# Half the memsets between gathers, one broadcast load of edge numbers, and 14 more kept blocks in a graph layer on one core

## The reference

```
edge_in_f = concat(h[src], h[dst], edge_attr)        # 192 wide
edge_in_r = concat(h[dst], h[src], edge_attr)
msgs_f = relu(edge_in_f @ W1_f + b1_f) @ W2_f + b2_f # 128 wide
msgs_r = relu(edge_in_r @ W1_r + b1_r) @ W2_r + b2_r
agg = segment_sum(msgs_f, dst, N) + segment_sum(msgs_r, src, N)
out = x + h + relu(concat(agg, h) @ Wn1 + bn1) @ Wn2 + bn2
```

## Time and profile before

| | us |
|---|---|
| median of three runs | 1631.61 |
| lowest, highest | 1625.42, 1633.73 |
| the profiled execution | 1627.22 |
| its span, first to last instruction | 1625.5 |
| busy in it: PE, DVE, ACT, POOL | 1318.5, 972.4, 944.0, 1120.1 |

### The profile page before, as it was taken

The page is one execution under the profiler, slowest core; times in us unless marked ns, Lnnn a source line. Parts: engine busy times, 40 slices in busy tenths (PEclk is TensorE's granted clock), DMA queues, the critical chain, the costliest instruction groups (busy, mean ns, idle before and its releaser), DMA issues.

```text
span 1625.5 us, 29085 instructions
## 1 busy us (share of the span) xinstructions
PE 1318.5 (81%) x7070; PEld 997.1 (61%) x7070; DVE 972.4 (60%) x2902; ACT 944.0 (58%) x2256; POOL 1120.1 (69%) x1003
## 2 busy tenths in 40 slices
PE   6988998457787788887877887878888865899998
PEld 4777776345565666665656665656666654666665
DVE  7999998336666666666665666666666641222222
ACT  5888888244555455555545555455555533677776
POOL 7899878888888888888888888888888862000000
PEclk9999999567878777778787778787777777999999
DMA  7999998335555555555545555555555546999998
GB/s 222 310 312 315 315 312 280 101 59 108 103 109 108 107 104 103 102 103 103 102 93 99 101 103 102 98 100 102 103 103 102 102 76 205 333 369 348 346 349 292
DMA packets 238374, 280.71 MB, mean 173 GB/s; under 512 B 53170, under 2 KB 155200, under 8 KB 238348
## 3 DMA queue, kind: packets, MB, share of 16 engines
q1 hardware_dynamic: 168408, 241.57, 44.7%
q0 software_dynamic: 68992, 38.59, 20.3%
q10 hardware_dynamic: 948, 0.30, 0.1%
HBM read 162.62 MB, written 117.72 MB: 172 GB/s over the span
## 4 chain that ended last, share of the span: by engine, by line
POOL 28%; issue 19%; DMA 15%; PE 9%; DVE 5%; ACT 1%; POOLq 0%; SPq 0%; DVEq 0%; another core or an unknown queue 0%; ACTq 0%
POOL table L532 24%; DMA out_x<-ncentred 12%; POOL got_odd L514 5%; DMA table<-to_send,scatter_at 3%; PE bank L846 3%; DVE ncentred L1137 2%; PE bank L820 2%; PE bank L818 2%; PE bank L833 1%; DVE same L979 1%; PE bank L871 1%; DMA same<-table 1%; PE bank L804 1%; PE bank L882 0%; DVE sums L961 0%
## 5 line engine op out<-in xcount | busy, mean ns | idle before, releaser
L532 POOL DMA_INDIRECT table<-to_send,scatter_at x392 | 640.9, 1635 | 134.1 <-issue 118.3
L846 PEld LDWEIGHTS bank<-message,same 128*128 128x128 f32 x1960 | 300.1, 243 | 47.1 <-issue 43.6
L846 PE MATMUL bank<-message,same 128*128 128x128 f32 x1960 | 322.4, 335 | 3.3 <-DVE message L1010 3.3
L639 ACT ACTIVATE nh<-nx,all_sums,all_rstd 128x64 f32<-128x64 f32 x784 | 280.2, 434 | 0.0
L514 POOL DMA_INDIRECT got_even<-in_x,gather_first x196 | 211.8, 1081 | 40.9 <-issue 36.1
L775 PE MATMUL bank<-wn_h,nturned 128*128 128x256 f32 x784 | 196.6, 394 | 26.9 <-ACT nhidden L683 18.4
L514 POOL DMA_INDIRECT got_odd<-in_x,gather_at x180 | 179.9, 999 | 54.8 <-issue 54.2
L818 PE MATMUL bank<-turned,w_ends 128*128 128x256 f32 x392 | 175.5, 540 | 37.8 <-ACT turned_edge L609 37.1
L804 PE MATMUL bank<-ident,h_ends 128*128 128x128 f32 x196 | 51.4, 355 | 184.4 <-DVE h_ends L1019 181.4
L1004 DVE TENSOR_TENSOR scatter_at<-moved,ids 128x4 int32<-128x4 f32 x98 | 16.0, 163 | 296.6 <-DMA table<-to_send,scatter_at 296.6
L775 PEld LDWEIGHTS bank<-wn_h,nturned 128*128 128x128 f32 x784 | 143.1, 192 | 63.3 <-issue 33.0
(11 more groups left out here) (78 smaller groups left out, 1971.0 us busy)
## 6 DMA issues: line engine op xcount, KB each, us to landing
nx<-in_x SPq DMA_DIRECT2D x194, 256.0 KB
table<-nhidden SPq DMA_DIRECT2D x97, 512.0 KB
same<-table SPq DMA_DIRECT2D x97, 512.0 KB, 5.3
others<-numbers SPq DMA_DIRECT2D x196, 128.0 KB
out_x<-ncentred SPq DMA_DIRECT2D x97, 256.0 KB, 4.4
nx<-out_x SPq DMA_DIRECT2D x55, 256.0 KB, 4.6
out_x<-nh SPq DMA_DIRECT2D x31, 256.0 KB
table<-to_send,scatter_at POOLq DMA_INDIRECT x392
```

The lines of the kernel that those rows point to most:

```text
L532: pool.indirect_dma_start(table, bass.IndirectOffsetOnAxis(ap=scatter_at[s][:, k:k + 1], axis=0), to_send[s][:, k, :], None, compute_op=AL ...
L639: last = act.activation(nh[s][:, g, :], nx[place][:, g, :], ACT.Relu, bias=all_sums[:, at, g:g + 1].rearrange("p a g -> p (a g)"), scale=a ...
L846: last = pe.matmul(bank[6 + s][:, k * M:(k + 1) * M], same[s][:, o, k * P:(k + 1) * P], message[s][:, o, :], start=(o == k), stop=(o == KB ...
```

## The change

Three things change, and buffers are laid over each other to make room.

- Pauses: the memset stands only behind every second gather of those issued ahead, 104 times in place of 208, and `copy_sums` waits for 104.
- Edge numbers: `numbers` is laid out tile by tile, the 128 sources and then the 128 targets of each tile, so that a batch's row is 512 numbers in one piece; `others` is loaded by one DMA of 256 KB in place of two of 128 KB.
- Kept blocks: place 3 as before (24), place 1 for all 24 full turns, place 2 for turns 16 to 23 (THIRD = 8): 56 windows. Stored and loaded again are 42: place 0 (25), place 2 for turns 0 to 15, and window 97.
- Buffers: `kept_more` grows from 18 to 32 slots of 2 KB per partition. For room, ncentred, nsquares, nturned and the rows for `table` (now `nrows`) lie in slots 12 to 21 of it in the first stage, and `zeros` in slots 8 and 9. In the third stage nhidden, nbiased (nturned before) and nout lie over buffers of the second stage. ends_int and ends_row lie over others[1] and message[0], for which SP waits once more (`s_rowf`).

```
-    MORE = 18
-    MORE_FROM = KEPT - MORE
+    THIRD = 8
+    THIRD_FROM = KEPT - THIRD
...
-    numbers = nc.dram_tensor("numbers", (2, NT * P), I32, kind="Internal").ap()
+    numbers = nc.dram_tensor("numbers", (NT, 2, P), I32, kind="Internal").ap()
...
-        nxh = [nh[2], nh[3], nsquares[0]]
+        nxh = [nh[2], nh[3], nh[3]]
...
-        kept_more = sb("kept_more", [P, MORE, G * D])
-        zeros = kept_more[:, 0:2, :].rearrange("p a c -> p (a c)")[:, 0:ZC]
-        nturned = two("nturned", [G // 2 * P])
-        nhidden = two("nhidden", [G * P])
-        nout = ncentred
+        kept_more = sb("kept_more", [P, KEPT + THIRD, G * D])
...
+        zeros = kept_more[:, 8:10, :].rearrange("p a c -> p (a c)")[:, 0:ZC]
+        ncentred = [kept_more[:, 12 + s, :].rearrange("p (g d) -> p g d", d=D) for s in range(2)]
+        nsquares = [kept_more[:, 14 + s, :].rearrange("p (g d) -> p g d", d=D) for s in range(2)]
+        nturned = [kept_more[:, 16 + s, :] for s in range(2)]
+        nrows = [kept_more[:, 18 + 2 * s:20 + 2 * s, :].rearrange("p a c -> p (a c)") for s in range(2)]
...
         def in_ring(w, k):
 
-            place = w.of(NRING, k)[1]
-            return not (place == NRING - 1 or place == 1 and MORE_FROM <= w.least(k) // NRING < KEPT)
+            place, turn = w.of(NRING, k)[1], w.least(k) // NRING
+            return place == 0 or place == 1 and turn >= KEPT or place == 2 and turn < THIRD_FROM
...
-                for end in (SRC, DST):
-                    sp.dma_start(others[s][:, :, end, :],
-                                 numbers[end:end + 1, bass.ds(first_edge, JT * P)]
-                                 .rearrange("a (j p) -> a j p", p=P).to_broadcast([P, JT, P])
-                                 ).then_inc(s_others[s], 16)
+                sp.dma_start(others[s][:, :, :, :].rearrange("p j e q -> p (j e q)"),
+                             numbers.rearrange("(a t) e p -> a (t e p)", a=1)
+                             [:, bass.ds((2 * i + s) * (KB * P), KB * P)].to_broadcast([P, KB * P])
+                             ).then_inc(s_others[s], 16)
...
                     sp.wait_ge(s_numbers, 32)
+                    sp.wait_ge(s_rowf, 1)
                     load(0, 0)
...
                     else:
                         continue
+                    if k % 2 == 0:
+                        continue
                     if pauses:
                         pool.wait_ge(s_paused, pauses)
                     pool.memset(idle, 0.0).then_inc(s_paused, 1)
...
                 elif s == 0:
-                    act.wait_ge(s_paused, KB * (PAIRS + LOOK))
+                    act.wait_ge(s_paused, KB // 2 * (PAIRS + LOOK))
...
-                    if not first(turn):
-                        dve.wait_ge(e_stored[place], 16 * (turn - skipped(w, k)))
+                    if place == 1:
+                        dve.wait_ge(e_stored[2], 16 * THIRD_FROM)
+                    elif not first(turn):
+                        dve.wait_ge(e_stored[place], 16 * turn)
```

More of the change, by code:

```diff
@@ L166, in gnn_layer @@
         sums = two("sums", [KB])
-        centred = two("centred", [KB, D])
-        squares = two("squares", [KB, D])
+        moments = two("moments", [2, KB, D])
+        centred = [moments[s][:, 0, :, :] for s in range(2)]
+        squares = [moments[s][:, 1, :, :] for s in range(2)]
         var = two("var", [KB])
@@ L183, in gnn_layer @@
         to_send = two("to_send", [KB, M])
+        ends_int = others[1][0:TB, :, :, :]
+        ends_row = message[0][0:TB, :, :].rearrange("p (e b) q -> p e b q", b=2)
         nx = [sb(f"nx{p}", [P, G, D]) for p in range(NRING)]
@@ L191, in gnn_layer @@
         all_rstd = sb("all_rstd", [P, NW, G])
-        ncentred = two("ncentred", [G, D])
-        nsquares = two("nsquares", [G, D])
         nvar = two("nvar", [G])
@@ L196, in gnn_layer @@
         nh = [sb(f"nh{p}", [P, G, D]) for p in range(NRING)]
-        nxh = [nh[2], nh[3], nsquares[0]]
+        nxh = [nh[2], nh[3], nh[3]]
         idle = to_send[0][:, 0:2, :].rearrange("p k m -> p (k m)")
-        kept_more = sb("kept_more", [P, MORE, G * D])
-        zeros = kept_more[:, 0:2, :].rearrange("p a c -> p (a c)")[:, 0:ZC]
-        nturned = two("nturned", [G // 2 * P])
-        nhidden = two("nhidden", [G * P])
-        nout = ncentred
+        kept_more = sb("kept_more", [P, KEPT + THIRD, G * D])
[4 more added lines that the diff above has]
+        nrows = [kept_more[:, 18 + 2 * s:20 + 2 * s, :].rearrange("p a c -> p (a c)") for s in range(2)]
+        nhidden = [[to_send[s][:, :, :].rearrange("p k m -> p (k m)"),
+                    moments[s][:, :, :, :].rearrange("p a k d -> p (a k d)")] for s in range(2)]
+        nbiased = [hidden[s][:, :, :].rearrange("p a b -> p (a b)") for s in range(2)]
+        nout = [message[s][:, :, :].rearrange("p k (h d) -> p (k h) d", d=D) for s in range(2)]
         s_params = sem("params_in")
@@ L349, in set_up @@
                 for end in (SRC, DST):
-                    sp.dma_start(numbers[end, :].rearrange("(b t p) -> t b p", b=2, p=P),
+                    sp.dma_start(numbers[:, end, :].rearrange("(b t) p -> t b p", b=2),
                                  ends_int[:, end, :, :]).then_inc(s_numbers, 16)
@@ L410, in store_rows @@
                 sp.wait_ge(b_rows[s], 2 * (i + 1))
-                store_window(table[0:N, :], i, s, nhidden[s][:, :], b_stored[s])
+                store_window(table[0:N, :], i, s, nrows[s], b_stored[s])
             def begin(w):
@@ L450, in batch @@
                 store_xh(w, -1)
-            run(sp, NB, [(4, MORE_FROM * NRING, 4), (MORE_FROM * NRING, 92, 4)], 1, batch)
+            run(sp, NB, [(4, THIRD_FROM * NRING, 4), (THIRD_FROM * NRING, 92, 4)], 1, batch)
             def load_xh(w, k):
@@ L471, in store @@
                 store_window(out, i, s, flat(nout[s]), n_stored[s])
-            for place, turns in ((0, KEPT + 1), (1, KEPT + 1 - MORE), (2, KEPT)):
+            for place, turns in ((0, KEPT + 1), (1, 1), (2, THIRD_FROM)):
                 sp.wait_ge(e_stored[place], 16 * turns)
@@ L675, in copy_begin @@
                     act.wait_ge(b_product[s], i)
-                act.copy(nturned[s][:, :], bank[s][:, :]).then_inc(b_turned[s], 1)
+                act.copy(nturned[s], bank[s][:, :]).then_inc(b_turned[s], 1)
             def copy_rows(half):
@@ L682, in copy @@
                         act.wait_ge(b_stored[s], 16 * i)
-                    act.copy(nhidden[s][:, half * 512:(half + 1) * 512], bank[2 + 2 * s + half][:, :]
+                    act.copy(nrows[s][:, half * 512:(half + 1) * 512], bank[2 + 2 * s + half][:, :]
                              ).then_inc(b_rows[s], 1)
@@ L719, in add_bias @@
                     act.wait_ge(n_back[s], i)
-                act.activation(nturned[s][:, :], bank[s][:, :], ACT.Identity,
+                act.activation(nbiased[s], bank[s][:, :], ACT.Identity,
                                bias=bn2_col[:, 0:1]).then_inc(n_biased[s], 1)
@@ L882, in layer2_nodes @@
                         last = pe.matmul(bank[s][odd * D:(odd + 1) * D, c:c + 256], wn2[:, :],
-                                         nhidden[s][:, odd * 512 + c:odd * 512 + c + 256], start=True, stop=True)
+                                         nhidden[s][odd][:, c:c + 256], start=True, stop=True)
                 last.then_inc(n_l2[s], 1)
@@ L891, in turn_back @@
                 for q in range(G // 2):
-                    last = pe.transpose(bank[6 + s][:, q * P:(q + 1) * P], nturned[s][:, q * P:(q + 1) * P], ident[:, :])
+                    last = pe.transpose(bank[6 + s][:, q * P:(q + 1) * P], nbiased[s][:, q * P:(q + 1) * P], ident[:, :])
                 last.then_inc(n_back[s], 1)
```

23 lines of the change are left out of this document (11 added, 12 removed).

## The result

| | us |
|---|---|
| kernel before, median of 4 runs | 1629.58 (1625.42 to 1633.73) |
| changed kernel, median of 4 runs | 1816.10 (1811.87 to 1818.96) |
| ratio | 1.114, 95% interval 1.110 to 1.118 |
| profiled execution of the changed kernel | 1811.87, span 1810.1 |

The forecast was 1594. The changed kernel is 11% slower, outside the range and in a way that none of the rivals had. That is half of the result. The other half came with the last runs: **the same file, not altered by a letter, took 1590.34 us when it was run again, on chip 5** (4 runs, 1585.76 to 1593.63, against 1628.39 there; ratio 0.977, 0.975 to 0.979). The chip of the first measurement is not on record.

What follows compares the result with a forecast made beforehand. VectorE paces the first stage, POOL's queue the edge stage, DMA engines are 0.95 busy in the last; POOL's pauses delay the first scatter. Pauses 31.6 plus loads 5.7 save 37.3 us: 1594.3 us from the 1631.61 median, range 1582 to 1612.

Steps and rivals of the forecast that it cites:

- Part 1: First stage, POOL's gathers issued ahead: 208 memsets become 104, saving 31.6 us (19.8 pauses, 11.8 gathers hit less often).
- the pauses "0" below: Lower bound on the halved pauses' gain: 0 if the gap between gathers in the first stage is 0.49 us.
- Rival D: First stage: paired gathers block VectorE's two-input instructions, 0.48 us each, delaying the join; 50 us slower, 1682 us; chance 0.04.
- Gaps of 0.30 us, pauses at 0.19 us net: First-stage gathers: a pause occupies 0.49 us, 0.30 remains without it, so 104 removed pauses save 19.8 us.
- Gathers that meet VectorE: First stage: gathers lengthened by a running VectorE instruction are hit less often with the new step, saving 11.8 us.
- the walk: Gathers stepped along VectorE's recorded instructions: last pause ends at 307.4 us with the new sequence, 339.0 with the old.
- the bound of 37.3 us: Most that the pauses can give: first join done at 302.0 us, last pause ends at 339.3.
- Merged load: 0: Edge stage: 196 issues of 128 KB become 98 of 256 KB, hidden behind POOL, costed at nothing.
- 14 more kept blocks: 5.7: Last stage: 13 loads fewer at 0.44 us each save 5.7 us, bounds 2 and 13.4; the 14 stores saved give nothing.
- the forecast's quarter load (0.109): Last stage: a quarter of a load less per window is worth 0.109 us, from paces of 2.712 and 2.603 us.

Runs made afterwards that it cites:

- i1_changed_again: The changed kernel, not altered, run again in a later group on chip 5: 1590.34 us, ratio 0.9767 to the kernel before.
- e2_half_only: The kernel before with only the pauses halved (memset behind every second gather issued ahead), on chip 9: 1598.05 us, ratio 0.9788.
- h4_best: The changed kernel without pauses, edge ends in own buffers, 54 blocks kept, on chip 5: 1590.34 us, ratio 0.9757 to the kernel before.
- e1_all_pauses: The changed kernel with the memset again behind every gather (208), all other edits left in, on chip 9: 1626.76 us, ratio 0.9972 to the kernel before.
- i2_half_again: The kernel before with only the pauses halved, run again beside the changed kernel on chip 5: 1597.64 us, ratio 0.9805.
- f3_none: The changed kernel with no pause at all behind the gathers issued ahead, on chip 8: 1844.72 us (one run), stalled.
- f4_short_all: The changed kernel with a short memset (128x8) behind every gather, on chip 8: 1820.82 us, ratio 1.116 to the kernel before, stalled.

## Why the prediction was right and wrong

**The step that failed** in the measurement on record is the end of Part 1: "VectorE, TensorE and the loads have already gone as far as they can. The stage behind is the same chain started 31.6 us earlier." It priced a pause by POOL's time alone (0.49 us, 0.19 net) and took the first join to be done at 302 us whatever POOL does. In the stalled trace that join was done at 521.97 us, because the windows before it waited for TensorE's held increments, and the first scatter came at 523.45 us, not 309. In the trace of before, with 0.49 us behind every gather, no increment of TensorE was late in the first stage; that the pauses were the reason is argued, not shown, since half of them did no harm on chips 9 and 5. The trace of before could not give that price; but the prediction bounded the pauses "0" below, without asking whether a gap on one engine is a resource of another. **Rival D** had the right question (gathers in pairs block an engine of the first stage) and the wrong engine, VectorE, with a price from its own instructions. They didn't lengthen: 681 and 696 ns before, 681 and 706 in i1_changed_again, 683 and 697 for those that ran in the first 277 us of the stalled trace, means of the two groups of two-input instructions. The Trainium skill's rule (SBUF — State Buffer, Who interferes with whom), read as D reads it, that a GpSimd instruction which starts first holds up VectorE's, isn't seen in any of them; the other direction, a gather held up by VectorE, is the earlier trace rows. What D lacked is that an engine can be blocked between its instructions, in the signal that it is done.

Term by term, with i1_changed_again beside the kernel before (spans 1584.0 and 1625.5, so 41.5 us; forecast 37.3):

- **Gaps of 0.30 us, pauses at 0.19 us net: right.** The last pause ended 37.8 us sooner (339.3 to 301.5), of which the gathers' own time, below, is 18.1; 19.7 are left for the pauses, where 19.8 were forecast. The timeline of the end of the gathers:

```profile
298.69 1.07 POOL L525 DMA_INDIRECT got_even<-in_x,gather_first  x1 [0.16 <-issue]
300.06 0.97 POOL L525 DMA_INDIRECT got_even<-in_x,gather_first  x1 [0.30 <-issue]
300.27 2.50 PE L859 MATMUL bank<-message,same 128*128 128x128 f32 x20
...
301.03 0.45 POOL L580 MEMSET to_send<- 128x256 f32 x1
...
302.80 0.59 ACT L638 COPY to_send<-bank 128x512 f32<-128x512 f32 x1 [1.28 <-PE bank L859]
...
304.25 1.64 POOL L543 DMA_INDIRECT table<-to_send,scatter_at  x1 [2.77 <-issue]
```

- **Gathers that meet VectorE: too small, and by another way.** The group of first gathers:

```profile
L525 POOL DMA_INDIRECT got_even<-in_x,gather_first x196 | 194.8, 994 | 54.7 <-issue 49.2
```

The mean fell from 1081 to 994 ns, 208 x 0.087 = 18.1 us where the walk gave 11.8. The prediction had gathers "hit less often". They are hit nearly as often, 61 of 208 start inside a two-input instruction where it was 67, but later in it, and last 1.08 us on average, not 1.34. So POOL is done at 301.5 us, not 307.4, and the copy no longer waits for it but for the join (302.77): the bound of 37.3 us is nearly used up, and the first scatter comes 36.6 us earlier (340.86 to 304.25; forecast 31.6). (In e2_half_only the last pause, at 305.1 us, still sets it: first scatter at 306.6.) That is also why taking the remaining 104 pauses away brings little: h4_best without any takes the same 1590.3 us, its first scatter at 305.8.
- **Merged load: 0, right.** First to last batch 1004.6 us against 1006.2, most periods 10.2 to 10.8 as before. Over all traces that stretch lies between 1004.2 and 1011.2 us, with the merged load and without.
- **14 more kept blocks: 5.7, borne out by the times, not readable from a pair of traces.** The kernels that differ in the pauses not at all, but in the kept blocks and the other edits, are 5.5 us apart (e1_all_pauses and the kernel before; 1.6 to 7.3 by the interval) and 7.3 us (i1_changed_again and i2_half_again). In the traces the first output to the last took 253.0 us where it was 256.3, 3.4 us less (e1_all_pauses: 2.4), but that stretch varies as much from trace to trace: 254.2 to 259.3 us in the seven traces with 42 blocks kept, 252.7 to 258.5 in the seven with 56 (means 256.7 and 255.0). From output 8 to 24 the pace went from 2.712 to 2.606 us a window, which looks like the forecast's quarter load (0.109), yet five other traces with 56 blocks have 2.55 to 2.72 there. Outputs 24 to 96 came at 2.595 for 2.603, 64 to 96 at 2.55 where 2.49 was forecast. VectorE still waits 173.9 us for its output stores there:

```profile
DVE message L1152 <- DMA out_x<-message: 173.9, 90, 3.9
```

The page's DMA rows have the loads as counted, 41 for the forecast 42, and packets fell from 238374 to 195141:

```profile
others<-numbers SPq DMA_DIRECT2D x98, 256.0 KB, 3.7
...
nx<-out_x SPq DMA_DIRECT2D x41, 256.0 KB, 4.6
```

The medians of the last group, 1628.39 and 1590.34, differ by 38.0 us. Where no increment is held the sum comes out, and in part by luck: in this pair of traces the gathers gave 5.0 us more than forecast, the loads 2.3 less and the edge stage 1.6 that nobody forecast. The number on record was wrong by 222 us.

No version here is shown to beat both kernels everywhere. The changed kernel and h4_best save 2.4% where nothing is held back; the changed kernel costs 11% where it is. e1_all_pauses saves 0.3% with all pauses kept, on the one chip where it ran.

## What to carry to other kernels

A delay that someone wrote into an engine's queue may be protecting another engine, and no row of the trace with the delay in place says so: before pricing its removal by the time it takes, say which signals of other engines pass meanwhile, and measure the removal on more than one chip. When variants that can't differ do differ, lay the runs out by chip and time before looking for a cause in the code, and run the kernel that showed the effect again beside each group of variants; here that came only at the end, and four groups of variants were read without it. And where the profile says "remote", compare when the semaphore was raised with the end of the instruction that raises it.

## What the runs showed of the hardware that was not expected

- TensorE's semaphore increments can come up to 47 us late while GpSimd issues indirect DMAs of 0.96 us with gaps of 0.30 and 0.49 us in turn (up to 84 us with gaps of 0.30 us alone, f3_none); they are let go in order, and all at once after some 3 us without one (208.49 to 208.70 us, 304.46 and 304.52). GpSimd's own came up to 3.8 us late in the stalled trace. ScalarE's and VectorE's aren't held (0.01 us at the most from 3 us on).
- Whether it happens differs between two sets of executions of one program, 1811.87 to 1818.96 us (chip not recorded) and 1585.76 to 1593.63 us (chip 5), four runs each. The kernel before, 1625 to 1634 us in every group, shows nothing of it in its times.
- It is steady where it occurs (the four runs of f4_short_all lie within 0.8%), and comes back within 9 us after all has been let go (208.70, then 1.5 us late at 217.57 and 10 at 233.59). In the edge stage, with six scatters and gathers in a batch of 10.4 us, it isn't seen: there the stalled trace has 13 increments late by 0.7 to 1.9 us, and the trace before has 13 of 0.6 to 1.9.
